# One VectorE operation per half for the gate, and a residual sum prepared by GpSimd, at the end of a graph and LSTM kernel

## The chip, the cores and the metric

The kernel runs on one core of a Trainium2 chip. The metric is the device time of one execution in microseconds; the median of three runs of the kernel before is 2620.16 us (2617.37 to 2628.99). The core has five engines that work side by side and wait for each other through semaphores: TensorE (PE, matrix products into the memory called PSUM), VectorE (DVE) and ScalarE (ACT) for elementwise work, GpSimd (POOL), and SyncE (SP), which here issues DMA transfers.

## The reference

The input x has 6250 rows (nodes, later the time steps of one sequence) of 256 features. It is normalised, passed through a graph layer and a linear attention, and the residual sum x1 comes out. Then an LSTM of 256 units runs over the 6250 rows and gives H. What matters here is what follows the LSTM:

```
lstm_out = _lstm(x, W_ih, W_hh, b_ih, b_hh)                 # H, 6250 x 256
logits = einsum('bth,lh->btl', lstm_out, W_lin) + b_lin     # two logits a row
g = argmax(logits, axis=-1)                                 # 0 or 1
w = g * lstm_out
inc = cumsum(w, axis=1)
prefix, suffix = inc - w, inc[:, -1:, :] - inc
out = x1 + 2.0 * lstm_out + prefix * fw_att + suffix * bw_att
```

With two logits the argmax is 1 exactly where the second logit is greater than the first.

## The kernel before, in words

**Layout.** From the residual sum on, everything is kept with features on partitions: 256 features are two halves c = 0, 1 of 128 partitions. x1 lies in bufC (`x1T`, [128, half, row]). The LSTM cuts the 6250 rows into CH = 125 chunks of LS = 50 steps, runs all chunks at once and sweeps again until the states at the chunk borders agree. Its states lie in bufB as `hs` [128, step, half, chunk], so one step of all chunks is contiguous, while consecutive rows of one chunk are 250 elements apart. The sweeps end at L1582.

**The three stages that follow**, all written out by hand with semaphores, in blocks of BN = 250 rows, NB = 25 blocks, with buffers in pairs:

1. *Gates.* DVE copies the four columns of W_lin over 128 columns each (`lin_rep`, L1586), so that PE's product gives each logit on all partitions. Block i covers the steps 2i and 2i+1 of all chunks. PE (`logits`, L801 to L808) makes 2 logits x 2 halves, 4 products of 250 columns, into PSUM bank 6 or 7; a product in f32 is two matmul instructions in the trace. ACT (L1069 to L1073) moves the first logit with its bias to `lg0`. DVE (`gate`, L1589 to L1597) makes `gsel` = (second logit + bias > lg0) in one scalar_tensor_tensor (L1591), waits for it, and multiplies each half of H by it into `cum` (bufA; L1594, written with a stride of 50 elements so that `cum` is in the order of the rows), and waits for that too. PE may overwrite a bank when L1591 of two blocks earlier is done (`lg_g`).
2. *Scans.* Two running sums over 6250 elements, one a half, on DVE (L1603), and their last column times bw_att (L1607).
3. *Results.* Block i now covers 250 consecutive rows. DVE (`results`, L1610 to L1624): per half 2*H + x1 (L1614, H read with a stride), per half + cum*fw_att (L1620), then + the suffix term for both halves (L1624). ACT makes the suffix term (L1088) one block ahead and moves transposed blocks from PSUM to `outs` (L1096, in wq or wk). PE (`rows`, L818 to L824) transposes in four matmuls. SP (L391) stores 250 rows x 256 features with one DMA of 250 KB from 125 partitions. ACT may overwrite wq or wk when the store of two blocks earlier has landed (`out_st0`, `out_st1`).

GpSimd's last work before these stages is a cast of weights (L473), and nothing of its own follows.

Of the kernel before, what the change touches and what calls it, by code (L numbers as in the profile page):

```python
# [19 lines left out]
BN = 250  # L20
NB = N // BN
# [23 lines left out]
LS = 50  # L45
# [12 lines left out]
def build(nc, a, out):  # L58
# [7 lines left out]
    with ExitStack() as ctx:  # L66
        def sb(name, cols, dt=F32, parts=P):
            return ctx.enter_context(nc.sbuf_tensor(name, [parts, cols], dt))
# [16 lines left out]
        cum = bufA[:, 0:2 * (N + 1)].rearrange("p (c n) -> p c n", c=2)  # L85
# [5 lines left out]
        hs = bufB[:, 0:(LS + 1) * HC].rearrange("p (t c j) -> p t c j", c=2, j=CH)  # L91
# [3 lines left out]
        x1T = bufC[:, 0:2 * N].rearrange("p (c n) -> p c n", c=2)  # L95
# [15 lines left out]
        wih, whh = wx[:, 0:2 * G4], wx[:, 2 * G4:4 * G4]  # L111
# [34 lines left out]
        ones = sb("ones", P)  # L146
# [4 lines left out]
        fwc, bwc = cols[:, 8:10], cols[:, 10:12]  # L151
        blc = cols[:, 12:14]
        nbw, tbw = sb("nbw", 2), sb("tbw", 2)
        lin_c = sb("lin_c", 4)
        lin_rep = wih[:, 0:4 * P].rearrange("p (a m) -> p a m", a=4)
        bias_b = sb("bias_b", 3 * P, BF16, 8)[:, :].rearrange("p (a n) -> p a n", a=3)
        bias24 = sb("bias24", P, BF16, 24)
        sel24 = sb("sel24", 8 * CH, BF16, 24)
# [10 lines left out]
        scr = sb("scr", 3072)  # L169
# [29 lines left out]
        pre_kept = [[w[:, 0:2 * HC].rearrange("p (g n) -> p g n", g=2) for w in pair] for pair in ((wq, wk), (wv, wp))]  # L199
        dif = rs_buf[:, 1616 + G4:1616 + G4 + 4 * (CH - 1)].rearrange("p (a j) -> p a j", a=4)  # L200

        lg0, gsel = [scr[:, v * BN:(v + 1) * BN] for v in range(2)], scr[:, 512:512 + BN]
        suf, res = part[2:4], part[4:6]
        outs = [w[0:TP, :].rearrange("p (t d) -> p t d", d=D) for w in (wq, wk)]

        psum = ctx.enter_context(nc.psum_tensor("psum", [P, 8, 512], F32))
# [13 lines left out]
        def bank(b, c=2, w=BN, parts=P):  # L220
# [14 lines left out]
            "st_v", "g_mm", "i_mm", "f_mm", "o_mm", "si_act", "sf_act", "so_act", "prod_v", "c_v", "th_act", "h_v",  # L235
            "sw_d", "sw_v", "cnt_mm", "cnt_z", "flag_v", "w_low", "pre_mm", "kept_v", "pre_st0", "pre_st1", "pre_ld0", "pre_ld1",
            "hif_mm", "hgo_mm", "hif_act", "htg_act", "hc_v", "hth_act", "hh_v", "fill_a", "fill_d",
            "pe_swept", "lin_v", "lg_mm", "lg_act", "lg_g", "lg_v", "cum_v", "suf_act", "t_v", "out_mm", "out_act", "out_st0", "out_st1")}
        ld_x = [sem(f"ld_x{v}") for v in range(XR)]


# [159 lines left out]
        def _(pool):  # L401
# [69 lines left out]
            pool.wait_ge(S["y2_ps"], NB)  # L471
            for c in range(2):
                pool.tensor_copy(whb[c], whhv[:, c, :]).then_inc(S["w_low"], 1)  # L473


        @block.tensor
        def _(pe):
            mm = pe.matmul
            pe.wait_ge(S["ident_ok"], 1)
            pe.wait_ge(S["ld_w"], 48)  # L480
            for n, (blocks, _) in enumerate(groups):
                for j, b in enumerate(blocks):
                    last = pe.transpose(psum[:, 4 + n, j * P:(j + 1) * P], b, ident[:, :])
# [6 lines left out]
            for i in range(NT + 2):  # L490
                if i < NT:
                    t = i
# [3 lines left out]
                    for c in range(2):  # L496
                        last = pe.transpose(bank(2 + t % 2, 2, TP)[:, c, :], xr(t)[:, c * P:(c + 1) * P], ident[0:TP, 0:TP])
                    last.then_inc(S["xt_ps"], 1)
                if 1 <= i <= NT:
                    t = i - 1  # L500
# [34 lines left out]
            for h in range(2):  # L535
# [3 lines left out]
                last = pe.transpose(psum[:, 3, h * P:(h + 1) * P], ksum[:, h * P:(h + 1) * P], ident[:, :])  # L539
            last.then_inc(S["ctx_ps"], 1)  # L540

            for i in range(NB + 2):
                if i < NB:
                    if i >= 2:
                        pe.wait_ge(S["q_act"], i - 1)
                    for m in range(2):
                        for k in range(2):
                            last = mm(bank(i % 2)[:, m, :], wqv[:, k, m * P:(m + 1) * P], xnT[:, k, i * BN:(i + 1) * BN],  # L548
                                      start=(k == 0), stop=(k == 1))
                    last.then_inc(S["q_ps"], 1)  # L550
                if 1 <= i <= NB:
# [8 lines left out]
                    for h in range(2):  # L560
                        last = mm(bank(4 + b % 2)[:, h, :], ksb[:, h, :], q_e[b % 2][:, h, :], start=True, stop=True)
# [236 lines left out]


            mm(psum[0:1, 5, 0:1], ones[:, 0:1], ones[:, 0:1], start=True, stop=True).then_inc(S["pe_swept"], 1)  # L800
            pe.wait_ge(S["lin_v"], 1)  # L801
            def logits(i, par, first):
                if not first:
                    pe.wait_ge(S["lg_g"], i - 1)
                for l in range(2):
                    for k in range(2):
                        last = mm(psum[:, 6 + par, l * BN:(l + 1) * BN], lin_rep[:, 2 * l + k, :],
                                  hs[:, ds(2 * i + 1, 2), k, :], start=(k == 0), stop=(k == 1))  # L808
                last.then_inc(S["lg_mm"], 1)
            logits(0, 0, True)  # L810
            logits(1, 1, True)
# [4 lines left out]


            def rows(i, par, first):  # L818
                pe.wait_ge(S["t_v"], 4 * i + 4)
                if not first:  # L820
                    pe.wait_ge(S["out_act"], i - 1)
                for t in range(2):
                    for c in range(2):
                        last = pe.transpose(psum[0:TP, par, t * D + c * P:t * D + (c + 1) * P],  # L824
                                            res[par][:, c, t * TP:(t + 1) * TP], ident[:, :])
                last.then_inc(S["out_mm"], 1)
# [9 lines left out]
        def _(act):  # L836
# [229 lines left out]
                act.reg_add(k_r_, kv, 1)  # L1066
                act.reg_mov(go, act.value_load(flag[0:1, 0:1], min_val=0, max_val=CH))

            def logits(i, par, first):  # L1069
                act.wait_ge(S["lg_mm"], i + 1)  # L1070
                if not first:
                    act.wait_ge(S["lg_g"], i - 1)
                fn(lg0[par], psum[:, 6 + par, 0:BN], ACT.Identity, bias=blc[:, 0:1]).then_inc(S["lg_act"], 1)  # L1073
            logits(0, 0, True)
            logits(1, 1, True)
            with act.Fori(1, (NB - 1) // 2) as r:
                for u in range(2):
                    logits(2 * r + u, u, False)
            logits(NB - 1, 0, False)

            act.wait_ge(S["cum_v"], 5)

            def suffix(i, par):

                if not isinstance(i, int) or i >= 2:
                    act.wait_ge(S["t_v"], 4 * i - 4)
                for c in range(2):
                    last = fn(suf[par][:, c, :], cum[:, c, ds(i * BN + 1, BN)], ACT.Identity, bias=tbw[:, c:c + 1],  # L1088
                              scale=nbw[:, c:c + 1])
                last.then_inc(S["suf_act"], 1)  # L1090
# [20 lines left out]
        def _(dve):  # L1111
# [471 lines left out]


            dve.wait_ge(S["pe_swept"], 1)
            dve.tensor_copy(lin_rep, lin_c[:, :].unsqueeze(2).broadcast_to([P, 4, P])).then_inc(S["lin_v"], 1)  # L1586
            dve.memset(cum[:, :, 0:1], 0.0).then_inc(S["cum_v"], 1)

            def gate(i, par, first):  # L1589
                dve.wait_ge(S["lg_act"], i + 1)  # L1590
                stt(gsel[:, :], psum[:, 6 + par, BN:2 * BN], blc[:, 1:2], lg0[par], ALU.add, ALU.is_gt).then_inc(S["lg_g"], 1)  # L1591
                dve.wait_ge(S["lg_g"], i + 1)
                for c in range(2):
                    last = tt(cum[:, c, 1:N + 1].rearrange("p (j t) -> p t j", t=LS)[:, ds(2 * i, 2), :],  # L1594
                              hs[:, ds(2 * i + 1, 2), c, :], gsel[:, :].rearrange("p (t j) -> p t j", t=2), ALU.mult)
                last.then_inc(S["lg_v"], 1)
                dve.wait_ge(S["lg_v"], i + 1)  # L1597
            with dve.Fori(0, (NB - 1) // 2) as r:
                for u in range(2):
                    gate(2 * r + u, u, False)  # L1600
            gate(NB - 1, 0, False)
            for c in range(2):
                dve.tensor_tensor_scan(cum[:, c, 1:N + 1], ones[:, 0:1].broadcast_to([P, N]), cum[:, c, 1:N + 1], 0.0,  # L1603
                                       ALU.mult, ALU.add).then_inc(S["cum_v"], 1)
            dve.wait_ge(S["cum_v"], 3)
            for c in range(2):
                ts(tbw[:, c:c + 1], cum[:, c, N:N + 1], bwc[:, c:c + 1], None, ALU.mult).then_inc(S["cum_v"], 1)  # L1607

# [1 line left out]
            def results(i, par, first):  # L1610
                if not first:
                    dve.wait_ge(S["out_mm"], i - 1)
                for c in range(2):
                    last = stt(res[par][:, c, :].rearrange("p (j t) -> p j t", t=LS),  # L1614
                               hs[:, 1:LS + 1, c, ds(i * (BN // LS), BN // LS)].rearrange("p t j -> p j t"), 2.0,
                               x1T[:, c, ds(i * BN, BN)].rearrange("p (j t) -> p j t", t=LS), ALU.mult, ALU.add)
                last.then_inc(S["t_v"], 1)
                dve.wait_ge(S["t_v"], 4 * i + 1)
                for c in range(2):
                    stt(res[par][:, c, :], cum[:, c, ds(i * BN, BN)], fwc[:, c:c + 1], res[par][:, c, :],  # L1620
                        ALU.mult, ALU.add).then_inc(S["t_v"], 1)
                dve.wait_ge(S["t_v"], 4 * i + 3)
                dve.wait_ge(S["suf_act"], i + 1)
                tt(res[par], res[par], suf[par], ALU.add).then_inc(S["t_v"], 1)  # L1624
            results(0, 0, True)
# [29 lines left out]
```

## Time and profile before

| | us |
|---|---|
| median of 3 runs | 2620.16 |
| the profiled execution | 2621.64 |
| its span | 2619.8 |
| of it: start to the end of the sweeps | about 2460.8 |
| gates | 56.4 |
| scans | 26.3 |
| results, to the end | 76.3 |

The profile has the busy time of each engine, the span in 40 slices, a chain of waits that ended last, groups of equal instructions, and the same for any stretch. All times of rows are microseconds from the start of the span unless marked ns. "PEclk" is the granted TensorE clock, 1.00 for 2.4 GHz and 0.50 for 1.2 GHz. "DMA share" is the mean busy share of the core's 16 DMA engines. In a timeline, "x2" after a row says that two instructions are merged in it; in brackets stands how long the engine was idle before and who released it.

### The profile page before, as it was taken

To read this page: it belongs to the slowest core of one execution; us is meant where nothing else is said; L and a number is where in the kernel's file an instruction comes from. 1 tells how busy PE (TensorE), PEld (TensorE's weight loads), DVE (VectorE), ACT (ScalarE), POOL (GpSimd) and SP (SyncE) were. 2 spreads that over 40 slices of the span, in tenths; PEclk is the share of its full clock that TensorE was granted. 3 is DMA by queue.
4 is the path that set the end of the run, shared out by engine and by line. 5 is a ranking of instruction groups with operands and counts; after the bars stand their busy time and mean duration, and the time that the engine had idled before them with its cause. 6 is when DMAs were issued, how large, how long until landed. Compare 5 with 4: busy or idle time off the path is not lost.

```text
span 2619.8 us, 46777 instructions
## 1 busy us (share of the span) xinstructions
PE 2320.9 (89%) x14935; PEld 1991.4 (76%) x14935; DVE 1777.3 (68%) x4078; ACT 1521.5 (58%) x2860; POOL 120.6 (5%) x121
## 2 busy tenths in 40 slices
PE   4688989999999999999898999998887887888844
PEld 2467977888888888888786888888887887888733
DVE  5756888777777777777477455556665666566688
ACT  2354438888888888888533444445554555555315
POOL 4232000000000000000000000000000000000000
PEclk9789999999999999999999999999999999999975
DMA  3222220000000000000331122223332332333103
GB/s 97 70 68 82 87 80 20 27 28 24 24 29 24 27 26 29 23 25 24 107 95 44 55 86 86 86 86 110 110 116 80 116 109 91 104 114 113 39 7 91
DMA packets 95187, 174.12 MB, mean 66 GB/s; under 512 B 8984, under 2 KB 69412, under 8 KB 94770
## 3 DMA queue, kind: packets, MB, share of 16 engines
q1 hardware_dynamic: 63378, 86.63, 10.0%
q10 hardware_dynamic: 28108, 81.19, 9.9%
q0 software_dynamic: 3584, 4.76, 0.7%
q8 instruction: 73, 1.20, 0.2%
q14 instruction: 44, 0.35, 0.0%
HBM read 114.14 MB, written 58.36 MB: 66 GB/s over the span
## 4 chain that ended last, share of the span: by engine, by line
PE 65%; DVE 12%; issue 7%; ACT 5%; ACTq 2%; DVEq 1%; DMA 0%; POOL 0%; POOLq 0%; SPq 0%
PE psum L605 22%; PE psum L600 11%; PE psum L755 9%; PE psum L715 8%; DVE scr L1533 3%; DVE scr L1531 2%; ACT scr L1014 2%; PE psum L723 2%; PE psum L657 2%; PE psum L667 2%; PE psum L711 2%; PE psum L548 1%; PE psum L571 1%; DVE scr L1529 1%; ACTq L1025 1%
## 5 line engine op out<-in xcount | busy, mean ns | idle before, releaser
L927 ACT ACTIVATE counts<-psum 125x500 fp32r<-125x500 f32 (+1 forms) x663 | 719.9, 1121 | 159.1 <-PE psum L600 157.1
L605 PE MATMUL psum<-halves,counts 125*125 125x512 f32 x2500 | 742.5, 417 | 2.1 <-ACT counts L927 2.0
L1381 DVE TENSOR_TENSOR wx<-rs_buf 128x500 bf16<-128x500 bf16 (+2 forms) x1326 | 641.8, 531 | 129.4 <-PE psum L600 72.6
L755 PE MATMUL psum<-bufB,wx 128*128 x4800 | 603.4, 283 | 91.0 <-DVE bufB L1535 81.8
L755 PEld LDWEIGHTS psum<-bufB,wx 128*128 128x128 f32 x4800 | 564.8, 193 | 129.4 <-issue 118.5
L605 PEld LDWEIGHTS psum<-halves,counts 125*125 125x125 f32 x2500 | 417.6, 186 | 59.2 <-issue 3.9
L600 PE MATMUL psum<-wx 128*125 128x250 bf16 x2550 | 398.5, 276 | 5.9 <-DVE wx L1381 5.6
L600 PEld LDWEIGHTS psum<-wx 128*125 128x125 bf16 x2550 | 319.9, 138 | 91.4 <-DVE wx L1381 9.0
L715 PE MATMUL psum<-bufA,wx 128*128 (+1 forms) x1600 | 234.5, 290 | 0.0
L715 PEld LDWEIGHTS psum<-bufA,wx 128*128 128x128 f32 x1600 | 196.5, 193 | 23.9 <-issue 0.9
L1014 ACT ACTIVATE scr<-scr 128x125 f32<-128x125 f32 x300 | 92.2, 307 | 168.3 <-DVE scr L1533 168.3
L1535 DVE TENSOR_TENSOR bufB<-scr 128x125 f32 (+1 forms) x300 | 87.1, 290 | 146.6 <-ACT scr L1014 146.6
L1529 DVE TENSOR_TENSOR scr<-scr 128x125 f32<-128x125 f32 x300 | 85.9, 286 | 91.9 <-ACT scr L1007 91.8
L1002 ACT ACTIVATE psum<-bufA 128x500 f32<-128x500 f32 x144 | 85.7, 595 | 95.5 <-ACT scr L1014 95.4
L1007 ACT ACTIVATE scr<-psum 128x250 f32<-128x250 f32 x300 | 110.2, 367 | 31.7 <-PE psum L755 31.7
L1488 DVE COPY bufB<-psum 128x250 f32<-128x250 f32 x192 | 75.2, 415 | 61.1 <-PE psum L715 58.9
L1523 DVE COPY psum<-bufA 128x500 f32<-128x500 f32 x144 | 97.7, 678 | 23.2 <-issue 23.1
L1533 DVE TENSOR_TENSOR scr<-scr 128x125 f32<-128x125 f32 x300 | 87.1, 290 | 10.3
L983 ACT ACTIVATE scr<-psum 128x250 f32<-128x250 f32 x50 | 19.0, 380 | 128.2 <-PE psum L723 128.2
L824 PE MATMUL psum<-ident,scr 128*125 128x128 f32 x100 | 30.3, 458 | 70.1 <-DVE scr L1624 70.1
L1531 DVE TENSOR_TENSOR scr<-scr 128x125 f32<-128x125 f32 x300 | 86.1, 287 | 5.6 <-ACT scr L1009 1.4
L1009 ACT ACTIVATE scr<-psum 128x125 f32<-128x125 f32 x300 | 81.7, 272 | 6.6 <-PE psum L755 1.4
(257 smaller groups left out, 2521.7 us busy)
## 6 DMA issues: line engine op xcount, KB each, us to landing
bufA<-gates_of_x ACTq DMA_DIRECT2D x144, 500.0 KB, 3.4
gates_of_x<-bufB SPq DMA_DIRECT2D x48, 500.0 KB, 2.6
sums_by_feature<-scr SPq DMA_DIRECT2D x51, 125.0 KB, 2.1
x_times_eps_plus_sums<-rs_buf ACTq DMA_DIRECT2D x10, 625.0 KB
wx<-in_x_dram SPq DMA_DIRECT2D x25, 250.0 KB
x_plus_mix<-wx SPq DMA_DIRECT2D x25, 250.0 KB, 4.8
scr<-x_times_eps_plus_sums SPq DMA_DIRECT2D x50, 125.0 KB
x_times_eps_plus_sums<-scr SPq DMA_DIRECT2D x50, 125.0 KB
```

The lines of the kernel that those rows point to most:

```text
L600: last = mm(psum[0:TP, u % 3, g * KEYS:(g + 1) * KEYS], oh_l[r][:, g, :, t], oh_m[r][:, g, :, t], start=(t == 0), stop=(t == 1))
L605: return mm(psum[0:TP, 3 + v, :], cnt[v][:, hi, :], xhl[:, hi, :, :].rearrange("p s d -> p (s d)"), start=(hi == 0), stop=(hi == NT - 1))
L715: last = mm(gate_bank(u, m), wihv[:, c, m * P:(m + 1) * P], ls_in[:, ds(t, 1), c, :].rearrange("p t j -> p (t j)"), start=False, stop=Fals ...
L755: return mm(half_gates(u, m, slot[0])[:, slot[1], :], whhv[:, k, (2 * gate + m) * P:(2 * gate + m + 1) * P], h, start=False, stop=(k == 1) ...
L927: fn(cnt[v][:, :, 2 * GW * u:2 * GW * u + GW * g].rearrange("p h c -> p c h"), psum[0:TP, u % 3, 0:g * KEYS].rearrange("p (c h) -> p c h", ...
L1007: fn(half(s_if, m), half_gates(u, m, 1), ACT.Sigmoid).then_inc(S["hif_act"], 1)
L1014: fn(th[:, m * CH:(m + 1) * CH], tg_c[1 - u][:, 1, m * CH:(m + 1) * CH], ACT.Tanh).then_inc(S["hth_act"], 1)
L1381: last = tt(to[:, 0:gs, :, :], tab2[:, 0:k, :].unsqueeze(1).broadcast_to([P, gs, k, 2]), keysT[v][:, part_, g0:g0 + gs, :].unsqueeze(2).br ...
L1523: dve.tensor_copy(fill_to(u, 1), gates[0].rearrange("p g (m j) -> p m g j", m=2)).then_inc(S["fill_d"], 1)
L1529: tt(prod[:, 1, cut], s_if[:, 1, cut], tg_c[u][:, 1, cut], ALU.mult)
L1531: tt(prod[:, 0, cut], s_if[:, 0, cut], tg_c[u][:, 0, cut], ALU.mult).then_inc(S["prod_v"], 1)
L1533: tt(tg_c[1 - u][:, 1, cut], prod[:, 0, cut], prod[:, 1, cut], ALU.add).then_inc(S["hc_v"], 1)
```

## The change

1. *One logit difference.* DVE makes `lin_d` = W_lin[1] - W_lin[0] and `b_d` = b_lin[0] - b_lin[1], and copies only `lin_d` over the columns. PE makes one product per half, 2 a block where there were 4. The gate is (difference > b_d).
2. *Gate and product in one.* Per half one scalar_tensor_tensor with a pointer scalar: (PSUM is_gt b_d) mult H into `cum`. ACT's copy, `lg0`, `gsel` and the waits inside the block go. PE may overwrite a bank when both halves of two blocks earlier are done (`lg_v`).
3. *Scans* take their factor 1.0 from a PSUM column (`psum[:, 4, 0:1]`, set by a memset) in place of `ones` in SBUF.
4. *GpSimd* waits until the sweeps are over, and then adds H twice to x1 in place: 25 blocks x 2 rounds x 2 halves = 100 tensor_tensor adds of 250 elements. The second round of a half waits for its first.
5. *Results* start with cum*fw_att + x1T (with a wait for GpSimd's four adds of this block), so L1614 goes.

```
+            pool.wait_ge(S["pe_swept"], 1)
+            for i in range(NB):
+                cells = x1T[:, :, i * BN:(i + 1) * BN].rearrange("p c (j t) -> p c j t", t=LS)
+                for r in range(2):
+                    for c in range(2):
+                        if r:
+                            pool.wait_ge(S["xh_q"], 4 * i + c + 1)
+                        pool.tensor_tensor(cells[:, c, :, :], cells[:, c, :, :],
+                                           hs[:, 1:LS + 1, c, i * (BN // LS):(i + 1) * (BN // LS)].rearrange("p t j -> p j t"),
+                                           ALU.add).then_inc(S["xh_q"], 1)
...
-                    pe.wait_ge(S["lg_g"], i - 1)
-                for l in range(2):
-                    for k in range(2):
-                        last = mm(psum[:, 6 + par, l * BN:(l + 1) * BN], lin_rep[:, 2 * l + k, :],
-                                  hs[:, ds(2 * i + 1, 2), k, :], start=(k == 0), stop=(k == 1))
+                    pe.wait_ge(S["lg_v"], i - 1)
+                for k in range(2):
+                    last = mm(psum[:, 6 + par, 0:BN], lin_rep[:, k, :], hs[:, ds(2 * i + 1, 2), k, :],
+                              start=(k == 0), stop=(k == 1))
...
-                fn(lg0[par], psum[:, 6 + par, 0:BN], ACT.Identity, bias=blc[:, 0:1]).then_inc(S["lg_act"], 1)
...
-            dve.tensor_copy(lin_rep, lin_c[:, :].unsqueeze(2).broadcast_to([P, 4, P])).then_inc(S["lin_v"], 1)
+            tt(lin_d[:, :], lin_c[:, 2:4], lin_c[:, 0:2], ALU.subtract).then_inc(S["lin_v"], 1)
+            tt(b_d[:, :], blc[:, 0:1], blc[:, 1:2], ALU.subtract).then_inc(S["lin_v"], 1)
+            dve.wait_ge(S["lin_v"], 2)
+            dve.tensor_copy(lin_rep, lin_d[:, :].unsqueeze(2).broadcast_to([P, 2, P])).then_inc(S["lin_v"], 1)
             dve.memset(cum[:, :, 0:1], 0.0).then_inc(S["cum_v"], 1)
+            dve.memset(psum[:, 4, 0:1], 1.0).then_inc(S["cum_v"], 1)
...
-                dve.wait_ge(S["lg_act"], i + 1)
-                stt(gsel[:, :], psum[:, 6 + par, BN:2 * BN], blc[:, 1:2], lg0[par], ALU.add, ALU.is_gt).then_inc(S["lg_g"], 1)
-                dve.wait_ge(S["lg_g"], i + 1)
+                dve.wait_ge(S["lg_mm"], i + 1)
                 for c in range(2):
-                    last = tt(cum[:, c, 1:N + 1].rearrange("p (j t) -> p t j", t=LS)[:, ds(2 * i, 2), :],
-                              hs[:, ds(2 * i + 1, 2), c, :], gsel[:, :].rearrange("p (t j) -> p t j", t=2), ALU.mult)
+                    last = stt(cum[:, c, 1:N + 1].rearrange("p (j t) -> p t j", t=LS)[:, ds(2 * i, 2), :],
+                               psum[:, 6 + par, 0:BN].rearrange("p (t j) -> p t j", t=2), b_d[:, 0:1],
+                               hs[:, ds(2 * i + 1, 2), c, :], ALU.is_gt, ALU.mult)
                 last.then_inc(S["lg_v"], 1)
-                dve.wait_ge(S["lg_v"], i + 1)
...
-                dve.tensor_tensor_scan(cum[:, c, 1:N + 1], ones[:, 0:1].broadcast_to([P, N]), cum[:, c, 1:N + 1], 0.0,
+                dve.tensor_tensor_scan(cum[:, c, 1:N + 1], psum[:, 4, 0:1].broadcast_to([P, N]), cum[:, c, 1:N + 1], 0.0,
...
+                dve.wait_ge(S["xh_q"], 4 * i + 4)
                 for c in range(2):
-                    last = stt(res[par][:, c, :].rearrange("p (j t) -> p j t", t=LS),
-                               hs[:, 1:LS + 1, c, ds(i * (BN // LS), BN // LS)].rearrange("p t j -> p j t"), 2.0,
-                               x1T[:, c, ds(i * BN, BN)].rearrange("p (j t) -> p j t", t=LS), ALU.mult, ALU.add)
-                last.then_inc(S["t_v"], 1)
-                dve.wait_ge(S["t_v"], 4 * i + 1)
-                for c in range(2):
-                    stt(res[par][:, c, :], cum[:, c, ds(i * BN, BN)], fwc[:, c:c + 1], res[par][:, c, :],
+                    stt(res[par][:, c, :], cum[:, c, ds(i * BN, BN)], fwc[:, c:c + 1], x1T[:, c, ds(i * BN, BN)],
                         ALU.mult, ALU.add).then_inc(S["t_v"], 1)
-                dve.wait_ge(S["t_v"], 4 * i + 3)
+                dve.wait_ge(S["t_v"], 3 * i + 2)
```

## Rows read from the trace of the kernel before

**Rows 1.** The page: PE's and POOL's busy time, the granted clock in 40 slices

```profile
span 2619.8 us, 46777 instructions
...
PE 2320.9 (89%) x14935; PEld 1991.4 (76%) x14935; DVE 1777.3 (68%) x4078; ACT 1521.5 (58%) x2860; POOL 120.6 (5%) x121
...
PEclk9789999999999999999999999999999999999975
```

**Rows 2.** Windows of the three stages: length, busy PE, PEld, DVE, ACT, POOL, PEclk, DMA share, GB/s

```profile
2460.80:2517.20 56.40, 50.10 (x200) 37.47 (x200) 39.77 (x77) 11.75 (x25) 0.00 (x0) 0.95 0.00 0
2517.20:2543.50 26.30, 0.00 (x0) 0.00 (x0) 26.25 (x3) 0.00 (x0) 0.00 (x0) 0.50 0.00 0
2543.50:2619.80 76.30, 30.35 (x100) 22.97 (x100) 63.91 (x127) 39.22 (x75) 0.00 (x0) 0.50 0.28 84
```

**Rows 3.** Timeline of one pair of gate blocks: start, us, what

```profile
2469.79 0.48 DVE L1591 SCALAR_TENSOR_TENSOR scr<-psum,cols,scr 128x250 f32<-128x250 f32 x1 [0.42 <-DVE bufA L1594]
2470.51 1.09 DVE L1594 TENSOR_TENSOR bufA<-bufB,scr 128x250 f32 x2 [0.25 <-DVE scr L1591]
...
2473.97 0.48 DVE L1591 SCALAR_TENSOR_TENSOR scr<-psum,cols,scr 128x250 f32<-128x250 f32 x1 [0.42 <-DVE bufA L1594]
...
2474.62 3.90 PE L807 MATMUL psum<-bufB,wx 128*128 x16 [0.28 <-DVE scr L1591]
```

**Rows 4.** Timeline of the first gate block

```profile
2460.80 0.43 DVE L1586 COPY wx<-lin_c 128x512 f32<-128x512 f32 x1 [1.59 <-PE psum L800]
...
2461.28 13.06 PE L807 MATMUL psum<-bufB,wx 128*128 128x250 f32 x48 [0.52 <-DVE wx L1586]
2465.02 0.47 ACT L1073 ACTIVATE scr<-psum,cols 128x250 f32<-128x250 f32 x1 [9.66 <-PE psum L807]
```

**Rows 5.** DVE groups from 2455 us on: busy us, mean ns, idle before

```profile
L1594 DVE TENSOR_TENSOR bufA<-bufB,scr 128x250 f32 x48 | 26.3, 633 | 6.0 <-DVE scr L1591 6.0
...
L1614 DVE SCALAR_TENSOR_TENSOR scr<-bufB,bufC 128x250 f32 x44 | 23.7, 582 | 0.0
L1620 DVE SCALAR_TENSOR_TENSOR scr<-bufA,cols,scr 128x250 f32<-128x250 f32 x50 | 21.7, 476 | 3.0
L1624 DVE TENSOR_TENSOR scr<-scr 128x500 f32<-128x500 f32 x25 | 17.0, 679 | 2.8
L1591 DVE SCALAR_TENSOR_TENSOR scr<-psum,cols,scr 128x250 f32<-128x250 f32 x25 | 11.9, 478 | 10.5 <-DVE bufA L1594 4.7 <-ACT scr L1073 4.4
...
L1565 DVE TENSOR_TENSOR rs_buf<-bufB 128x248 f32<-128x248 f32 x1 | 0.4, 418 | 0.0
```

**Rows 6.** GpSimd's adds (ns min/median/max), and DVE work beside them in two timelines

```profile
L440 POOL TENSOR_TENSOR scr<-scr x50: 719/727/1704, 42.4 to 222.6; 125x256 f32<-125x256 f32 x50
L434 POOL TENSOR_TENSOR halves<-wx,scr x8: 2887/2906/3804, 39.6 to 215.0; 125x1280 fp32r<-125x1280 f32 x8
206.28 3.36 POOL L440 TENSOR_TENSOR scr<-scr 125x256 f32<-125x256 f32 x4
207.15 0.43 DVE L1292 SCALAR_TENSOR_TENSOR scr<-psum,scr 125x256 f32<-125x256 f32 x1 [2.59 <-POOL scr L440]
95.55 0.72 POOL L440 TENSOR_TENSOR scr<-scr 125x256 f32<-125x256 f32 x1 [1.53 <-DVE scr L1292]
95.73 1.23 DVE L1237 TENSOR_TENSOR bufB<-bufB,tab 101x640 bf16<-101x640 f32 x1
```

**Rows 7.** The stores: issues (ns; first and last start), the last pair, and two DMA windows

```profile
L391 SPq DMA_DIRECT2D out_dram<-wq x13: 263/264/301, 2548.5 to 2615.4; - x13
2610.09 0.26 SPq L391 DMA_DIRECT2D out_dram<-wq  x1
2614.76 0.60 ACT L1096 ACTIVATE wq<-psum 125x512 f32<-125x512 f32 x1 [2.21 <-DMA out_dram<-wq]
2555.00:2605.00 50.00, 21.54 (x72) 16.23 (x71) 45.38 (x91) 27.86 (x54) 0.00 (x0) 0.50 0.31 92
199.50:204.00 4.50, 4.50 (x25) 3.87 (x24) 2.34 (x5) 2.09 (x5) 0.59 (x2) 1.00 0.34 119
```

More of the change, by code:

```diff
@@ L154, in build @@
         lin_c = sb("lin_c", 4)
-        lin_rep = wih[:, 0:4 * P].rearrange("p (a m) -> p a m", a=4)
+        lin_rep = wih[:, 0:2 * P].rearrange("p (a m) -> p a m", a=2)
+        lin_d, b_d = sb("lin_d", 2), sb("b_d", 1)
         bias_b = sb("bias_b", 3 * P, BF16, 8)[:, :].rearrange("p (a n) -> p a n", a=3)
@@ L200, in build @@
         dif = rs_buf[:, 1616 + G4:1616 + G4 + 4 * (CH - 1)].rearrange("p (a j) -> p a j", a=4)
-        lg0, gsel = [scr[:, v * BN:(v + 1) * BN] for v in range(2)], scr[:, 512:512 + BN]
         suf, res = part[2:4], part[4:6]
@@ L237, in build @@
             "hif_mm", "hgo_mm", "hif_act", "htg_act", "hc_v", "hth_act", "hh_v", "fill_a", "fill_d",
-            "pe_swept", "lin_v", "lg_mm", "lg_act", "lg_g", "lg_v", "cum_v", "suf_act", "t_v", "out_mm", "out_act", "out_st0", "out_st1")}
+            "pe_swept", "lin_v", "lg_mm", "lg_v", "xh_q", "cum_v", "suf_act", "t_v", "out_mm", "out_act", "out_st0", "out_st1")}
         ld_x = [sem(f"ld_x{v}") for v in range(XR)]
@@ L800, in _ @@
             mm(psum[0:1, 5, 0:1], ones[:, 0:1], ones[:, 0:1], start=True, stop=True).then_inc(S["pe_swept"], 1)
-            pe.wait_ge(S["lin_v"], 1)
+            pe.wait_ge(S["lin_v"], 3)
             def logits(i, par, first):
                 if not first:
-                    pe.wait_ge(S["lg_g"], i - 1)
-                for l in range(2):
-                    for k in range(2):
-                        last = mm(psum[:, 6 + par, l * BN:(l + 1) * BN], lin_rep[:, 2 * l + k, :],
-                                  hs[:, ds(2 * i + 1, 2), k, :], start=(k == 0), stop=(k == 1))
+                    pe.wait_ge(S["lg_v"], i - 1)
+                for k in range(2):
+                    last = mm(psum[:, 6 + par, 0:BN], lin_rep[:, k, :], hs[:, ds(2 * i + 1, 2), k, :],
+                              start=(k == 0), stop=(k == 1))
                 last.then_inc(S["lg_mm"], 1)
@@ L818, in rows @@
             def rows(i, par, first):
-                pe.wait_ge(S["t_v"], 4 * i + 4)
+                pe.wait_ge(S["t_v"], 3 * i + 3)
                 if not first:
@@ L1067, in _ @@
                 act.reg_mov(go, act.value_load(flag[0:1, 0:1], min_val=0, max_val=CH))
[L1069 to L1072, printed above, removed]
-                fn(lg0[par], psum[:, 6 + par, 0:BN], ACT.Identity, bias=blc[:, 0:1]).then_inc(S["lg_act"], 1)
[L1074 to L1081, printed above, removed]
+            act.wait_ge(S["cum_v"], 6)
             def suffix(i, par):
                 if not isinstance(i, int) or i >= 2:
-                    act.wait_ge(S["t_v"], 4 * i - 4)
+                    act.wait_ge(S["t_v"], 3 * i - 3)
                 for c in range(2):
@@ L1601, in _ @@
             gate(NB - 1, 0, False)
+            dve.wait_ge(S["lg_v"], NB)
             for c in range(2):
-                dve.tensor_tensor_scan(cum[:, c, 1:N + 1], ones[:, 0:1].broadcast_to([P, N]), cum[:, c, 1:N + 1], 0.0,
+                dve.tensor_tensor_scan(cum[:, c, 1:N + 1], psum[:, 4, 0:1].broadcast_to([P, N]), cum[:, c, 1:N + 1], 0.0,
                                        ALU.mult, ALU.add).then_inc(S["cum_v"], 1)
-            dve.wait_ge(S["cum_v"], 3)
+            dve.wait_ge(S["cum_v"], 4)
             for c in range(2):
```

## The prediction

> **What bounds the kernel now.** I read the page first: GpSimd works 5% of the span, so there is an idle engine [rows 1]. The change touches nothing ahead of 2460.8 us. So I took windows of the three stages that follow: gates 56.4 us, scans 26.3, results 76.3 [rows 2], 159 us of 2619.8. Nothing outside them can move by more than noise.
>
> In the gates the window shows two engines near their limit: PE is busy 50.1 of 56.4 us, DVE 39.8 [rows 2]. The timeline shows why both matter. A pair of blocks takes 2473.97 - 2469.79 = 4.18 us, 2.09 a block. DVE's part is serial: 0.48 for the comparison, 0.25 of waiting for its own result, 1.09 for two products, 0.13 to 0.42 of waiting. PE's 16 matmuls of a pair take 3.90 us, 1.95 a block [rows 3]. So removing DVE work alone would win 0.14 us a block; it needs PE's half too, which this change brings.
>
> The scans are DVE alone [rows 2]. In the results DVE is busy 45.4 of 50 us and everybody waits for it, but one wait for a store appears at the end, where the last blocks follow each other a little faster [rows 7]. That is the hidden second limit there.
>
> **Gates, part by part.** PE: 8 matmul instructions a block become 4, at 3.90/16 = 0.244 us each at the 2.4 GHz clock: 0.98 us. At 1.2 GHz the first block's 8 took 2465.02 - 2461.28 = 3.74 us [rows 4], so 4 take 1.87.
>
> DVE: one operation with PSUM and SBUF inputs, a pointer scalar and the strided write. No row has this form. Nearest rows: the strided product 633 ns [rows 5], with a spacing of 1.09 - 0.63 = 0.46 in a pair [rows 3]; the operation with a pointer scalar costs 476 or 478 ns against 418 for the plain one of the same length, 0.06 more, the same from PSUM and from SBUF [rows 5]. I take 0.69 with a spacing of 0.52, so a block is 1.21 and DVE could start one every 1.04. Bounds: 0.48 (stride free) and 0.85 an operation.
>
> The loop over two banks is PE 0.98, about 0.05 to DVE, DVE 1.21, 0.17 back to PE (2473.97 + 0.48 to 2474.62 [rows 3]): 2.41 for two blocks, 1.21 each. With 0.04 for loop turns that are not hidden, my estimate, I take 1.25 a block, bounds 1.05 and 1.6. ACT's 25 copies were in the chain only through their landing time and go.
>
> Start: two tiny subtractions, a wait and a copy half as long in place of one copy of 0.43: weights ready 0.2 us later, bounds 0 and 0.9 (GpSimd starts at the same moment, below). First gate at 2461.4 + 0.05 + 1.87 = 2463.4 us. The granted clock is 0.95 over the window, so at most 5.6 us of it are at 0.50 [rows 2]: low at first, high from about 2466. So two more blocks come at PE's 1.87, 1.2 us more. Scans start at 2463.4 + 25 x 1.25 + 1.2 + 0.2 = 2496.1 in place of 2517.2: **21.1 us won** (bounds 12 and 26).
>
> **Scans.** Same instruction, one input from PSUM. The PSUM and SBUF forms above agree within 2 ns, so 26.3 stays; bounds -0.5 and +0.5. Results start at 2496.1 + 26.3 + 0.3 = 2522.7.
>
> **Results, what DVE loses.** A block is now about 2.79 us: 25 stores are issued from 2548.5 to 2615.4, 24 intervals [rows 7]. Two operations of 582 ns with a wait go, DVE's block falls to two of 476 (0.39 apart) and one of 679: about 1.6 us. ACT has two suffix operations and a move, 1.7 us at most (39.2 busy us over 25 blocks is 1.57 [rows 2]); PE 1.2. If these were all, a block would cost 1.7 and the stage 27 us less. They are not.
>
> **The store takes over.** Each buffer is free again only when its store has landed: issue at 2610.09, ACT released at 2614.76, 4.67 us; with ACT's 0.60 and some 0.1 to SP's issue a buffer turns in 5.4 us, two blocks, 2.7 a block, against 2.79 now. And the DMA engines have little left: a share of 0.31 of 16 is 5.0 engines at 92 GB/s [rows 7]. The fastest that rows show for a transfer of the same form (125 partitions, 1 KB pieces) is 119 GB/s, again at 0.34 of 16 [rows 7]: 256,000 bytes at that rate are 2.15 us. So a block lies between 2.15 and 2.7, and as the last pair is near to what the stage would become I take 2.65. That is 24 x 0.14 = 3.4 us, and the first store comes 0.7 sooner (1.1 of DVE less, then the suffix term is late): 4.1 us won, bounds 2 and 12.
>
> The Trainium skill ("DMA: Bandwidth & Descriptors", Why a DMA increments its semaphore by 16 and not by 1) says that the number of engines is the largest up to 16 that divides the slowest dimension, for 125 partitions 5. The trace agrees, 0.31 x 16 = 5.0. By it a shorter DVE block can't raise the ceiling.
>
> **GpSimd's 100 adds.** A free-standing add of 256 elements takes 727 ns, and 1280 elements 2906 [rows 6], so 250 elements are about 0.72. H is read with a stride, as in L1614, where DVE's 582 against 476 bounds such a penalty; I take 0.73 an add, bounds 0.6 (two halves overlapped) and 1.2. From 2461 on: 73 us, finished at 2534. Results need block i at 2522.7 + 2.65i and GpSimd has it at 2461 + 2.9(i+1), so its order is early enough by itself.
>
> But beside GpSimd DVE is not free. A DVE operation with PSUM and SBUF inputs ran in 0.43 us amid four adds of GpSimd, as alone. One with two SBUF inputs (640 elements; from 679 ns for 500, some 0.82) took 1.23 us when it met an add that had 0.54 us to run [rows 5, 6]: it stood still until the add ended, but for a start-up of 0.13 that it could have meanwhile. The new gates and the new scans have one SBUF input: no cost. All three DVE operations of a result block have two. While GpSimd runs they alternate with its adds: 3 x 0.73 + 1.5 (three operations, some 0.45, 0.45 and 0.6 when start-up is hidden) = 3.7 us a block in place of 2.65. At 2522.7 GpSimd has done 61.7/0.73 = 84 adds; the 16 left go by in about 5.2 blocks, at 1.05 each: **5.4 us lost**.
>
> The Trainium skill ("SBUF — State Buffer", Who interferes with whom) says the same: two SBUF inputs contend with a GpSimd instruction that reads SBUF, the later one blocks until the first is done, and one SBUF input doesn't contend. It speaks against part 4 in the results and for parts 2 and 3. The trace agrees with it in the two cases above. With it the results lose the 5.4, without it nothing.
>
> **Sum** on the profiled execution (2621.64, span 2619.8): -21.1 - 4.1 + 5.4 = -19.8 us. Its own time is 1.5 above the median, so I take the difference to the median: 2620.16 - 19.8, **2600 us**.
>
> **Rivals.**
> A. *GpSimd is done, or harmless, when the results start.* Adds of 0.6 us end at 2522. For it: the two halves are independent, and the 727 includes start-up. Against: even contiguous adds are close to 0.7 apart. -25.2, 2595 us; with a store every 2.5 us, 2591.
> B. *PE's clock drops in the gates*, since PE has work for only 0.98 of 1.25 us. Then four matmuls take 1.87, a block about 1.95, scans start at 2512; GpSimd is then done before the results: -5 - 4.1, 2611 us. For: the clock is 0.5 in the results, where PE has 43% [rows 7]. Against: PE would be at work for 78% of each block, and the page shows the full clock through nearly all of the span, in which PE's busy share is 89% in the mean [rows 1].
> C. *GpSimd becomes the bound* (the other side). If a strided add takes p us, 61.7/p are done at 2522.7, and the (100 - 61.7/p)/3 contended blocks cost 3p + 1.5 - 2.65 each. p = 0.9 loses 16 (2611 us); p = 1.02 eats the whole 25.2; p = 1.1 loses 31: 2626 us; p = 1.2 loses 40: 2635 us. It decides from 1.02 us. For: no row shows GpSimd reading with a stride. Against: its rate of 2.1 ns an element leaves more room than DVE's.
> D. *The change doesn't do what it says in the results*: DVE's work there goes, and the time doesn't follow, because of the store. That is in the forecast.
>
> **How the numbers follow.** Forecast 55%, A 25%, B 8%, C 12% (5 of them at p from 0.9 to 1.15). From A with faster stores, 2591, to C at 0.9, 2610. Half a per cent, 13 us, is about what can be told from no change here. Faster by more: forecast and A, 0.80. Within 13 us: B and the milder C, 0.13. Slower by more, C with p near 1.2 or above: 0.07.
>
> **What would show it right or wrong.** Scans start near 2496 and PE's clock at 1.00 before them; the new DVE operation at 0.69 (mean) with no growth beside GpSimd; GpSimd's adds at 0.73, and longer after 2522; DVE's result operations for the first five blocks over 1 us each, and at 476 and 679 after that; then ACT waiting for the stores of wq and wk in nearly every block, stores 2.65 apart. It is wrong if ACT never waits for a store, if results go on at 2.0 us a block, if the contended blocks are more than eight, or if gates take over 1.6.

## The result, and the profile after

The changed kernel takes 2612.98 us (median of 20 runs, 2607.68 to 2620.12) against 2621.18 (20 runs, 2616.88 to 2628.99): ratio 0.9967, 95% interval 0.9959 to 0.9975. That is 8 us faster, where 20 were forecast, and slower than the 2591 to 2610 us that the forecast spanned.

The profiled execution has a span of 2606.4 us, 13.4 below the one before; 3.8 of these lie ahead of the change, in sweeps that it doesn't touch (they end at 2457.0 instead of 2460.8 us) and are the difference of two executions. After them the stages are these windows (length, busy PE, PEld, DVE, ACT, POOL, PEclk, DMA share, GB/s), the counterpart of [rows 2]; the third is part of the results stage.

```profile
2457.00:2494.60 37.60, 28.85 (x100) 18.05 (x100) 31.15 (x55) 0.00 (x0) 37.53 (x47) 0.94 0.00 0
2494.60:2520.90 26.30, 0.00 (x0) 0.00 (x0) 26.25 (x3) 0.00 (x0) 26.30 (x33) 0.53 0.00 0
2520.90:2538.90 18.00, 0.00 (x0) 0.00 (x0) 17.95 (x4) 2.06 (x4) 17.30 (x22) 0.50 0.00 0
2538.90:2606.40 67.50, 30.35 (x100) 22.98 (x100) 36.16 (x73) 37.07 (x71) 0.00 (x0) 0.50 0.30 95
```

Gates are 37.6 us (56.4 before), scans 26.3 (26.3), results 18.0 + 67.5 = 85.5 (76.3). So 18.8 us are won and 9.2 lost: 9.6, close to the 8.2 of the medians. The loss is in the third window: DVE is busy all of it with four instructions, and POOL nearly all of it. The timeline there (start, us, engine, line):

```profile
2521.18 17.69 DVE L1617 SCALAR_TENSOR_TENSOR scr<-bufA,cols,bufC 128x250 f32<-128x250 f32 x2
...
2537.35 0.85 POOL L482 TENSOR_TENSOR bufC<-bufC,bufB 128x250 f32<-128x250 f32 x1
2538.90 0.68 DVE L1621 TENSOR_TENSOR scr<-scr 128x500 f32<-128x500 f32 x1
2539.50 0.86 DVE L1617 SCALAR_TENSOR_TENSOR scr<-bufA,cols,bufC 128x250 f32<-128x250 f32 x2
```

The first pair of result operations, 0.86 us everywhere else, takes 17.69 and ends 0.7 us after GpSimd's last add. Here is how the durations of the two forms are spread (ns, min/median/max), and the groups of the gates and of ACT's moves:

```profile
L1617 DVE SCALAR_TENSOR_TENSOR scr<-bufA,cols,bufC x50: 467/474/17302, 2521.2 to 2596.6; 128x250 f32 x44, 128x250 f32<-128x250 f32 x6
L482 POOL TENSOR_TENSOR bufC<-bufC,bufB x100: 839/852/897, 2457.1 to 2537.3; 128x250 f32<-128x250 f32 x100
```

```profile
L1595 DVE SCALAR_TENSOR_TENSOR bufA<-psum,b_d,bufB 128x250 f32 x48 | 28.2, 673 | 6.4 <-PE psum L817 4.7 <-issue 0.6
...
L1094 ACT ACTIVATE wq<-psum 125x512 f32<-125x512 f32 x13 | 7.8, 597 | 26.5 <-PE psum L834 17.5 <-DMA out_dram<-wq 9.0
L1094 ACT ACTIVATE wk<-psum 125x512 f32<-125x512 f32 x12 | 7.2, 597 | 14.8 <-DMA out_dram<-wk 14.8
```

One operation out of 50 is at 17302 ns, the median at 474. The 100 adds take 81.1 us from first to last: 0.852 each, but 0.81 apart, so in the trace each begins some 0.04 us before the one before it ends; this is called an unbroken stream below. The gate's operation has 673 ns and doesn't grow beside the adds (671 without them, in e1 below). ACT now waits for stores 23 times, 23.8 us in all (before: once, 2.2 us [rows 7]).

### The profile page after: what moved, and what is told of

Read it like the earlier page. It is cut to its first block, busy times and chain, and to the rows that moved or that the text cites. A ratio compares the mean times of both kernels' runs of the same rounds, so it can differ in the third digit from the quotient of the medians.

```text
span 2606.4 us, 46447 instructions
## 1 busy us (share of the span) xinstructions
PE 2295.9 (88%) x14835; PEld 1970.6 (76%) x14835; DVE 1758.6 (67%) x4006; ACT 1509.0 (58%) x2835; POOL 201.6 (8%) x221
## 4 chain that ended last, share of the span: by engine, by line
PE 61%; DVE 14%; issue 8%; ACT 6%; DMA 2%; ACTq 2%; DVEq 1%; POOL 0%; SPq 0%; POOLq 0%
PE psum L616 22%; PE psum L611 11%; PE psum L766 8%; PE psum L726 8%; DVE scr L1531 3%; DVE scr L1529 2%; DMA out_dram<-wq 2%; ACT scr L1024 2%; PE psum L734 2%; PE psum L722 2%; DVE wp L1449 2%; PE psum L559 1%; PE psum L582 1%; DVE scr L1527 1%; ACTq L1035 1%
## 5 line engine op out<-in xcount | busy, mean ns | idle before, releaser
L482 POOL TENSOR_TENSOR bufC<-bufC,bufB 128x250 f32<-128x250 f32 x100 | 81.1, 852 | 1016.7 <-PE psum L811 1016.7
```

## The experiments

Each ran beside the kernel before on the same chip; the ratio is to that. "First contact" below is an operation on full tiles with two SBUF inputs that is the first such to meet GpSimd's adds. An operation "stands" when it takes far longer than it does alone.

The whole times carry a difference that has nothing to do with the edits: in the fourteen profiles the sweeps, which no edit touches, end between 2452.4 and 2464.9 us. So here are, from each profile, the microseconds from VectorE's first instruction after the sweeps to the end, and of these the results stage.

| kernel | sweeps to end | results |
|---|---|---|
| before | 159.0 | 76.3 |
| the change; again (e5) | 149.4; 149.4 | 85.5; 84.6 |
| e1, no adds | 139.2 | 76.3 |
| e2, adds alone | 178.1 | 73.0 |
| e3, serial adds | 139.9 | 76.5 |
| e4, 19 blocks | 134.3 | 69.5 |
| e6; e7 | 149.9; 149.5 | 85.1; 84.7 |
| e8, 19 blocks, stores cut | 121.3 | 56.5 |
| e9; e10, gaps | 138.9; 140.1 | 75.0; 75.3 |
| e11, contact ahead of the scans | 176.6 | 69.1 |
| e12, ScalarE doubles | 115.5 | 52.6 |

**e1_no_gpsimd: gates and scans as changed, no adds, results as before.**

```
-            pool.wait_ge(S["pe_swept"], 1)
-            for i in range(NB): ...            # the 100 adds
...                                             # results(): the lines of before
```

> The change without its GpSimd part: gates and scans as changed, results as before (2*H + x1 on VectorE). Both theories: gates take some 36 us (56.4 before, 37.6 changed, less 1.4 for the weights that no longer wait for GpSimd's first adds), results 76.3 as before: 20 us faster than before, about 2601 us, and so 12 us faster than the whole change. If the whole change is not slower than this, the loss is not GpSimd's.

Measured: 2602.2 us, ratio 0.9924 (0.9904 to 0.9944). Half of the change alone wins 20 us or so; the other half takes back more than half of that. The gates' first instructions show a cost of the adds that the forecast's sum left out; it had one only in its bounds. The copy of the weights takes, without and with the adds (e1, then the change):

```profile
L1577 DVE COPY wx<-lin_d 128x256 f32<-128x256 f32 x1 | 0.3, 293 | 0.0
```

```profile
L1587 DVE COPY wx<-lin_d 128x256 f32<-128x256 f32 x1 | 0.9, 907 | 0.0
L1585 DVE TENSOR_TENSOR b_d<-cols 128x1 f32<-128x1 f32 x1 | 0.8, 839 | 0.0
```

Both wait for one add each, 1.3 us together. Here, after one and two adds, VectorE did get in. The copy has a single SBUF input and waits all the same: it takes 0.91 us beside an add that is under way, and 0.29 in e3, where it begins in a gap between two adds:

```profile
2457.26 0.29 DVE L1587 COPY wx<-lin_d 128x256 f32<-128x256 f32 x1
```

**e2_adds_only: adds and shorter results; gates and scans as before.**

```
+            ...                                # the 100 adds, and results() of the change
...                                             # logits(), gate(), scans: the lines of before
```

> The GpSimd part alone: 100 adds and the shorter results, gates and scans as before, where the gate's product reads two tiles in SBUF (bufB and scr, neither of them the adds' target). Theory 'stream' (while GpSimd has its next add queued, a VectorE operation with two SBUF inputs gets no turn): the first product waits until the adds are over, some 81 us after the sweeps, +76 us, and results without any wait -9: 2688 us. Theory 'turns' (after each add VectorE gets in, as forecast): 50 products wait 0.7 us each, +35, -9: 2647 us. Theory 'data' (the wait in the results comes from reading the tile that GpSimd writes): the products run undisturbed, 2612 us.

Measured: 2641.2 us, ratio 1.0072 (1.0046 to 1.0098). All three numbers miss. The form of "turns" is right and "stream" and "data" are wrong here. DVE's first products and scans, and the groups:

```profile
2467.46 2.04 DVE L1605 TENSOR_TENSOR bufA<-bufB,scr 128x250 f32 x2 [0.29 <-DVE scr L1602]
2469.62 0.48 DVE L1602 SCALAR_TENSOR_TENSOR scr<-psum,cols,scr 128x250 f32<-128x250 f32 x1
2470.35 2.08 DVE L1605 TENSOR_TENSOR bufA<-bufB,scr 128x250 f32 x2 [0.25 <-DVE scr L1602]
```

```profile
L482 POOL TENSOR_TENSOR bufC<-bufC,bufB 128x250 f32<-128x250 f32 x100 | 123.8, 1276 | 1017.3 <-PE psum L811 1017.3
L1614 DVE TENSOR_TENSOR_SCAN bufA<-ones,bufA 128x6250 f32<-128x6250 f32 x2 | 27.3, 13669 | 0.0
```

Two products take 2.04 to 2.08 us in place of 1.09 [rows 3]: each waits for one add, from the first one on, which came 5.5 us after the adds had begun. The adds' mean of 1.28 us includes two of 13.7 us that stood for the length of a scan; their median is 1.09, where it is 0.85 in the change. The scan with its factor in SBUF costs 13.67 us beside the adds; in the kernel before, where nothing runs beside it, the same scan takes 13.17, as with the factor in PSUM (13.16). In the results this kernel's L1626 is the very operation that stood 17 us in the change, and it took turns at once:

```profile
2567.40 1.63 DVE L1626 SCALAR_TENSOR_TENSOR scr<-bufA,cols,bufC 128x250 f32<-128x250 f32 x2
2569.06 1.21 DVE L1630 TENSOR_TENSOR scr<-scr 128x500 f32<-128x500 f32 x1
2570.20 2.05 DVE L1626 SCALAR_TENSOR_TENSOR scr<-bufA,cols,bufC 128x250 f32<-128x250 f32 x2
```

So the same two instruction streams can go two ways. What differs is what came before: here VectorE and GpSimd had been taking turns since 2467 us. That this decides is a guess at this point.

**e3_serial_adds: each add waits for the one before.**

```
-                        if r:
-                            pool.wait_ge(S["xh_q"], 4 * i + c + 1)
+                        if i or r or c:
+                            pool.wait_ge(S["xh_q"], 4 * i + 2 * r + c)
```

> The change, but each GpSimd add waits for the one before it, so there is a gap of some 0.1 us between two adds (0.95 us each in place of 0.81, 96 us in all). 'Stream': the gap gives VectorE its turn, result blocks of about 4 us from 2521 us on, 11 of them, and the whole as the change, about 2613 us, but with no operation over 1.5 us. If the gap is no help: VectorE stands until about 2553, +15, 2628 us. 'Turns': as the first.

Measured: 2601.7 us, ratio 0.9926 (0.9902 to 0.9949). Every add is later and the kernel is 11 us faster than the change. The mechanism came as expected; the 2613 was too high, since I had put an alternating block at 4 us and it is 3.2:

```profile
2520.09 2.02 DVE L1617 SCALAR_TENSOR_TENSOR scr<-bufA,cols,bufC 128x250 f32<-128x250 f32 x2
2522.14 1.21 DVE L1621 TENSOR_TENSOR scr<-scr 128x500 f32<-128x500 f32 x1
2523.28 2.06 DVE L1617 SCALAR_TENSOR_TENSOR scr<-bufA,cols,bufC 128x250 f32<-128x250 f32 x2
```

**e4_split19: adds for 19 blocks, VectorE makes the first six in the old way.**

```
-            for i in range(NB):
+            for i in range(NB - 19, NB):
...
+                own = isinstance(i, int) and i < NB - 19      # results(): L1614 of before for these
```

> GpSimd adds for the last 19 blocks alone (76 adds, 62 us, over 2 us before the results start); VectorE makes the first 6 blocks in the old way, and its results stage is written out, not looped. 'Stream' and 'turns': no operation of the results meets an add; against the change -17 us, +2 for six longer blocks: 2598 us. If the wait in the results were for something else than GpSimd's adds it would stay, 2613 us.

Measured: 2591.9 us, ratio 0.9895 (0.9869 to 0.9921). With the adds over before the results start, nothing stands, and the stages after the sweeps take 15.1 us less than in the change, as expected. The wait was for the adds. This kernel's results are also written out instead of looped, but e11, looped and with its adds over too, has results of 69.1 us against 69.5 here, so the loop isn't what stood.

**e5_again, e6_plain_first, e7_immediate: is it chance, or the form of the operation?**

```
+            tt(part[1][:, 0, :], part[0][:, 0, :], part[0][:, 1, :], ALU.add)     # e6, ahead of results(0)
...
-                    stt(res[par][:, c, :], cum[:, c, ds(i * BN, BN)], fwc[:, c:c + 1], x1T[:, c, ds(i * BN, BN)],
+                    stt(res[par][:, c, :], cum[:, c, ds(i * BN, BN)], 0.001, x1T[:, c, ds(i * BN, BN)],      # e7
```

> The changed kernel once more, unaltered, for its profile. Its first result operation (two SBUF inputs and a pointer scalar) stood 17.3 us in the one profile, until GpSimd's adds were over, while with serial adds, and in the results of the kernel with the adds alone, the same operation alternates with them. Theory 'first contact' (an unbroken stream of adds keeps such an operation out until it ends): the same 17 us again, 2613 us. Theory 'chance' (it depends on the phase of that execution): it may alternate this time, and the time would then be near 2602 us.

> The change with one plain tensor_tensor of 250 elements (two SBUF inputs, no pointer scalar; its output is not used) ahead of the results. The gate's plain product got in after one add when it first met the adds (kernel with the adds alone). 'Pointer' (only the form with a pointer scalar is kept out by an unbroken stream): the plain one takes at most 1.2 us, breaks the stream, and the others alternate: result blocks of 3.2 us while adds last, 2603 us. 'Any' (whatever comes first stands): the plain one stands 17 us, 2613 us.

> The change with fw_att as the immediate 0.001 in place of the pointer scalar; the prefix term is left at that one factor. 'Pointer': the first result operation gets in after one add, alternation, 2603 us. 'Any' and 'first contact': it stands 17 us, 2613 us.

Measured: 2608.9 us (ratio 0.9951, 0.9932 to 0.9969), 2612.2 (0.9967, 0.9956 to 0.9979), 2612.1 (0.9968, 0.9954 to 0.9982). In all three the first contact stands until the adds end, whatever its form; one row of each:

```profile
2523.80 16.81 DVE L1617 SCALAR_TENSOR_TENSOR scr<-bufA,cols,bufC 128x250 f32<-128x250 f32 x2
```

```profile
2524.98 16.38 DVE L1622 TENSOR_TENSOR scr<-scr 128x250 f32<-128x250 f32 x1
```

```profile
2523.15 16.70 DVE L1617 SCALAR_TENSOR_TENSOR scr<-bufA,bufC 128x250 f32<-128x250 f32 x2
```

"Pointer" has fallen, and that the standing recurs is shown. What differs from e2 and e3 is the stream of adds: it had gaps in e3, was young in e2's gates, and in e2's results had just been taking turns with VectorE.

One thing was not varied. In the change, e5, e6, e7 and e11 below, the operation that stood began at nearly the same point of an add's cycle, from 0.02 us before an add's start to 0.13 us after it, while e2's first product, which got in, began 0.35 us after one. This point alone doesn't explain it, since the change's copy of the weights began 0.09 us after the start of an add and waited only for that one (it has one SBUF input, though); but whether it plays a part beside the stream's age, no run shows.

**e9_gap_per_block and e10_one_gap: gaps in the stream.**

```
+                if i:                          # e9; in e10: if i == 21
+                    pool.wait_ge(S["xh_q"], 4 * i)
```

> The change with one wait of GpSimd for its own last add at each new block, so one gap in every four adds (serial adds had one after each). 'Gap' (VectorE with two SBUF inputs gets in where the stream of adds has a gap, and not in an unbroken stream of long standing): the first result operation stands at most one block of adds, 3.3 us, and from then on, having broken the stream, VectorE alternates; no operation over 3.5 us, result blocks 3.2 us until the adds end, about 2602 us. If one gap in four is too rare: more than 5 us of standing, 2606 to 2613 us.

> The change with one single gap in the stream of adds, ahead of the 85th, some 3 us after the results start. 'Gap': the first result operation stands about 3 to 5 us instead of 17, and then VectorE and GpSimd alternate to the end of the adds without any further gap, as they do in the kernel with the adds alone; 2603 us. If alternation needs a gap each time, VectorE gets one operation in and stands again: 2612 us.

Measured: 2600.8 us (ratio 0.9924, 0.9903 to 0.9945) and 2605.1 (0.9936, 0.9919 to 0.9952). In e10 (first fence) the first pair of operations takes 4.47 us, in e9 (second) 2.11, and alternation follows in both:

```profile
2529.89 4.47 DVE L1619 SCALAR_TENSOR_TENSOR scr<-bufA,cols,bufC 128x250 f32<-128x250 f32 x2
2534.40 1.21 DVE L1623 TENSOR_TENSOR scr<-scr 128x500 f32<-128x500 f32 x1
2535.54 2.05 DVE L1619 SCALAR_TENSOR_TENSOR scr<-bufA,cols,bufC 128x250 f32<-128x250 f32 x2
```

```profile
2526.09 2.11 DVE L1619 SCALAR_TENSOR_TENSOR scr<-bufA,cols,bufC 128x250 f32<-128x250 f32 x2
```

One wait in GpSimd's program, with no other edit, cuts the standing from 17 to 3.5 us (the first operation alone), and the stages after the sweeps from 149.4 to 140.1 us. After it no gap is needed. GpSimd's last 16 adds in e10 are again without a gap, each beginning some 0.04 us before the one before it ends, and VectorE takes its turn between them:

```profile
2533.18 17.02 POOL L484 TENSOR_TENSOR bufC<-bufC,bufB 128x250 f32<-128x250 f32 x16
```

So the later turns need no gap at the moment of contact. What the one gap, or the one turn taken, leaves behind stays open.

**e11_contact46: a first contact ahead of the scans.**

```
+            tt(part[1][:, 0, :], part[0][:, 0, :], part[0][:, 1, :], ALU.add)
             dve.wait_ge(S["lg_v"], NB)
```

> The change with one plain tensor_tensor with two SBUF inputs ahead of the scans, when some 46 adds are done (the first contact in the kernel with the adds alone came after 7 adds and got in at once; in the change after 78 and never). 'Age' (a stream unbroken for long keeps VectorE out): it stands until all adds are over, 44 us, after which nothing meets an add: 2613 - 17 + 44 = 2640 us. If it gets in at once, only the results' start or the last part of the stream is special: 2613 or 2602 us.

Measured: 2636.5 us, ratio 1.0058 (1.0038 to 1.0078). It stood 44 us, until the adds were over, and nothing stood after it:

```profile
2496.94 43.97 DVE L1603 TENSOR_TENSOR scr<-scr 128x250 f32<-128x250 f32 x1
2540.83 13.17 DVE L1606 TENSOR_TENSOR_SCAN bufA<-psum,bufA 128x6250 f32<-128x6250 f32 x1
```

**e8_split19_wide: e4 with each store cut in two.**

```
-                sp.dma_start(out[ds(i * BN, BN), :].rearrange("(t p) d -> p t d", p=TP), outs[par])...
+                rows = out[ds(i * BN, BN), :].rearrange("(t p) d -> p t d", p=TP)
+                sp.dma_start(rows[0:112, :, :], outs[par][0:112, :, :])...
+                sp.dma_start(rows[112:TP, :, :], outs[par][112:TP, :, :])...
```

> As the kernel with 19 blocks on GpSimd (2592 us), but each store cut in two: partitions 0 to 111, and the last 13. By the Trainium skill ('DMA: Bandwidth & Descriptors', how many engines) that is 16 and 13 DMA engines in place of 5. If the five engines are what holds a block at 2.5 us, the stores land about 2 us sooner, ACT waits for none, and a block is 1.7 to 1.8 us by ACT's and VectorE's work: -14 us, 2578 us. Rival: the time of a store is its fixed part or the making of its descriptors, and nothing moves, or two issues cost more: 2590 to 2595 us.

Measured: 2584.7 us, ratio 0.9856 (0.983 to 0.9882), against e4's 0.9895; between those two kernels some 7 to 10 us, where 14 were expected, with intervals that overlap. In the profiles the sweeps ended 6.6 us later in e8, and its results stage is 56.5 us against 69.5, 13.0 less. Here is a window of 35 us of the results, of e4 and then of e8, and ACT's moves in e8. In e8 it begins 6.6 us earlier in the stage, so it still holds some of the longer first blocks:

```profile
2535.00:2570.00 35.00, 17.97 (x60) 13.61 (x60) 20.87 (x44) 22.09 (x44) 0.00 (x0) 0.50 0.32 104
```

```profile
2535.00:2570.00 35.00, 21.94 (x74) 16.63 (x74) 28.51 (x60) 26.73 (x53) 0.00 (x0) 0.50 0.46 132
```

```profile
L1096 ACT ACTIVATE wq<-psum 125x512 f32<-125x512 f32 x13 | 7.8, 597 | 11.1 <-PE psum L836 11.0
```

The DMA share goes from 0.32 (5.1 of 16 engines) to 0.46, PE makes 74 matmuls instead of 60, and no wait for a store is left. After ACT's last move the kernel ends 2.8 us later, where it was 4.7 in e4. So the store from 125 partitions on some 5 engines was the limit, which fits the rule that the prediction quotes from the Trainium skill ("DMA: Bandwidth & Descriptors", Why a DMA increments its semaphore by 16 and not by 1). No run cuts the store and leaves the number of engines, so the two are not told apart.

**e12_act_doubles: the version that all this points to.**

```
+            act.wait_ge(S["pe_swept"], 1)
+            for i in range(NB): ...
+                    last = fn(twice[i % 4][:, c, :]..., hs[:, 1:LS + 1, c, ...], ACT.Copy, scale=2.0)
...
+            pool.wait_ge(S["lin_v"], 3)
+            for i in range(NB):
+                pool.wait_ge(S["dbl"], i + 1)
+                pool.tensor_tensor(x1T[:, :, i * BN:(i + 1) * BN], x1T[:, :, i * BN:(i + 1) * BN], twice[i % 4],
+                                   ALU.add).then_inc(S["xh_q"], 1)
```

> The best version so far pointed to: ScalarE, idle in gates and scans, writes 2*H of each block, GpSimd adds it in one operation of 500 elements a block (25 adds, started only when the weights are ready), stores cut in two as before (112 and 13 partitions), all 25 blocks from GpSimd. The adds take some 25 x 1.3 us or ScalarE's 1.2 us a block, both over by 2495, long before the results. Against the kernel with 19 blocks and wide stores (2585 us): weights 1.4 us sooner, six result blocks about 1 us shorter: 2578 us. If a store or PE is now the limit: no gain in the blocks, 2583 us.

Measured: 2576.7 us, ratio 0.9837 (0.9821 to 0.9854): 36 us below the change, 44 below before. The 25 wide adds take 1.17 us each in the mean and are over long before the results:

```profile
L481 POOL TENSOR_TENSOR bufC<-bufC,wx 128x500 f32<-128x500 f32 x25 | 28.1, 1170 | 1018.4 <-ACT wx L1082 1018.4
L1082 ACT ACTIVATE wx<-bufB 128x250 f32<-128x250 f32 x50 | 27.2, 645 | 5.4 <-PE psum L809 5.4
```

## Why the prediction was wrong

*Gates: right, a little small.* Forecast 21.1 us won, measured 18.8. The new operation takes 673 ns (forecast 690). The weights came 1.2 us later than forecast because two VectorE operations each met an add; they were ready 1.4 us later than before, where the forecast's upper bound was 0.9. The rest is the loop: the change's four matmuls of a block span 1.11 us instead of 0.98, and a pair of blocks 2.71 us instead of 2.50 (25 blocks, +2.6), against which the slow start was dearer in the forecast than it was. PE's clock stayed up (0.94 over the window): rival B fell.

*Scans: right*, 26.3 us. What the PSUM factor spared shows in e2: with it in SBUF the scans meet the adds, 0.5 us more for each scan, and an add stands behind each.

*The store as the next limit: right.* ACT waits for a store in nearly every block. Forecast 2.65 us a block, measured (2601.8 - 2541.7)/24 = 2.50: 3.6 us more won. e8 bears out the cause: with each store cut in two, no wait is left.

*GpSimd's adds: the step that failed.* The duration was short: 0.73 forecast, 0.81 from one to the next; when the results started 21 adds were left and not 16. But the failed step is "while GpSimd runs they alternate with its adds", 5.4 us lost. In place of about 5 slower blocks there was one operation that stood 17.3 us, until the stream was over, 16.8 of them lost. The measured block of alternation (3.2 us, e3) would have made even the 21 adds cost only some 7 x 0.7 = 5 us, an estimate; e9, which alternates from the first operation on, has results of 75.0 us against 69.1 in e11, where no add is left, so 5.9. The price that the forecast gave to alternation was about right. It was the alternation that didn't happen. The two rows that the step rested on [rows 6] showed VectorE meeting a single add with nothing queued behind it; they said nothing of a stream of 78.

Of the page that I weighed there ("SBUF — State Buffer", Who interferes with whom, in the Trainium skill: the later one blocks until the first is done) the trace agrees where VectorE waits for one add (the change's first two operations, e2, e3, e9); in the unbroken stream VectorE was held not for one instruction but for 21, and in e11 for 54. The prediction also dropped a condition of that section: an instruction with one SBUF input is clear of GpSimd only outside the 2-port perf modes, and a copy is among those that can enter them. The gates' operation agrees (one SBUF input, 673 ns throughout), and the copy of the weights (one SBUF input, 0.91 us in place of 0.29) was not clear; which mode it ran in, no run shows.

The sum by its measured terms: -18.8 (gates) + 16.8 (standing) - 7.6 (the rest of the results, got by difference; 4.1 forecast) = -9.6. Against the forecast's -19.8 the gates gave 2.3 less and the adds cost 11.4 more; that the stores gave 3.5 more hid part of it, which was luck.

Shown by the runs: that the adds are what the operation waits for (e4, e11), that its form doesn't matter (e6, e7), that it recurs (e5), and that a single gap ends it and leads to alternation (e10; e9 has a gap in every block). Not settled: why. That GpSimd's adds follow each other without a gap isn't enough: e2's first contact got in after seven such adds, the change's first two after one and two, and in e10 sixteen more without a gap let VectorE in each time. Where between 7 adds (in) and 46 (out) the border lies, whether it is the age of the stream or also the point in an add's cycle at which VectorE comes, and what changes until then, wasn't tried.

## What to carry to other kernels

Beside a long run of GpSimd adds that read SBUF, give VectorE's two-input operations one input from PSUM, or end the run before the first operation with two SBUF inputs. If they must overlap, put a wait for GpSimd's own last instruction into its program shortly before or just after that point: the gap costs 0.13 us, its absence cost 17 and 44. Even then the alternation cost some 6 us for 24 adds, so ending the run early is better. When an engine's work is cut in a stage that ends in stores, count the DMA engines first: a store from 125 partitions kept 5 of 16 busy, and cutting it at 112 took away every wait for a store.

## What the runs showed of the hardware that was not expected

- VectorE with two SBUF inputs can be held out for a whole unbroken stream of GpSimd adds: 16.4 to 17.3 us in four profiles (the change twice, e6, e7), 43.97 us in e11, for operations that take under 0.5 us alone. One gap in the stream ended it (e10), and the adds that followed without a gap held nothing out.
- Alternating has its own price on both sides: VectorE's block of three operations 3.2 us in place of 1.6, GpSimd's adds 1.02 to 1.29 us in place of 0.85 (e10's last).
- A VectorE copy with one SBUF input was held by an add as well: 0.91 us in place of 0.29.
- A pointer scalar costs a VectorE scalar_tensor_tensor 60 ns: median 474 ns with it, 414 with an immediate (the change and e7).
